# The head of a fused transformer block: value branch on four partitions with a 4 KB load, its copies ahead of the weight casts, attention weights loaded one chunk later

## What is computed

```python
x = x + _L0_attn_a_ref(_layernorm(x), W, b)            # value of token 1, added to every token of its batch
x = x + _L0_ffn_ref(_layernorm(x), W_r, W_k, W_v, mu_r, mu_k)
x = x + _L0_attn_b_ref(_layernorm(x), Wq, bq, Wk, bk, Wv, bv, Wo, bo)
x = x + _L0_ffn_ref(_layernorm(x), W_r, W_k, W_v, mu_r, mu_k)

def _L0_attn_a_ref(x, W, b):
    v = jnp.einsum('btc,dc->btd', x, W) + b
    return jnp.broadcast_to(v[:, 1:2, :], (B, T, C))

def _L0_ffn_ref(x, ...):
    x_prev = x shifted by one token
    xr = mu_r * x + (1.0 - mu_r) * x_prev
    xk = mu_k * x + (1.0 - mu_k) * x_prev
    r = sigmoid(xr @ W_r.T);  k = square(relu(xk @ W_k.T))
    return r * (k @ W_v.T)
```

## Time and profile before

| | us |
|---|---|
| median of three runs | 1783.31 |
| lowest, highest | 1781.94, 1785.71 |
| the profiled execution, whole | 1786.81 |
| its span, first to last instruction | 1785.0 |
| PE busy | 1527.8 |
| DVE busy | 1496.1 |
| ACT busy | 1317.8 |
| POOL busy | 947.9 |

### The profile page before, as it was taken

How to read it: one execution, slowest core, us unless ns; L and a number is a source line. 1 busy time by engine, 2 the same in 40 slices (tenths; PEclk the granted TensorE clock), 3 DMA queues, 4 the chain that set the end, 5 groups by cost and what they waited for, 6 DMA issues and landing times. The chain is left out here.

```text
span 1785.0 us, 46651 instructions
## 1 busy us (share of the span) xinstructions
PE 1527.8 (86%) x16872; PEld 1150.4 (64%) x16872; DVE 1496.1 (84%) x4034; ACT 1317.8 (74%) x2413; POOL 947.9 (53%) x762
## 2 busy tenths in 40 slices
PE   2788865789998989999998989999898999857998
PEld 1677752556666656666666666666666666646887
DVE  3888834889989989999999989999998999826885
ACT  2678823787878768777877878787876877718996
POOL 0243333565656656666665656566665666402444
PEclk8899977989999999999999999999999999978999
DMA  5032211888999899999999999999989998951322
GB/s 191 24 101 74 81 62 47 150 147 151 179 160 178 145 168 162 177 163 161 176 168 167 163 171 170 164 174 170 176 149 170 159 173 154 161 126 49 119 95 84
DMA packets 738435, 252.62 MB, mean 142 GB/s; under 512 B 703776, under 2 KB 722976, under 8 KB 738208
## 3 DMA queue, kind: packets, MB, share of 16 engines
q1 hardware_dynamic: 736688, 248.45, 72.7%
q10 hardware_dynamic: 1520, 1.18, 0.2%
HBM read 48.25 MB, written 25.17 MB: 41 GB/s over the span
## 5 line engine op out<-in xcount | busy, mean ns | idle before, releaser
L1174 ACT ACTIVATE at_prob<-at_prob,at_top 128x256 f32<-128x256 f32 x1024 | 435.8, 497 | 109.0 <-DVE at_top L1042 103.8
L1042 DVE CUSTOM_DVE_ANT_0 at_prob<-at_s_ps,at_masks,pre_s_scale 128x256 f32<-128x256 f32 x1024 | 428.8, 479 | 19.5 <-PE at_s_ps L1392 4.3
L1298 PE MATMUL at_pr_ps<-at_xt,pre_w_h 128*128 128x512 f16 x1024 | 298.9, 384 | 22.5 <-DMA at_xt<-at_x_halves 19.9
L1053 DVE TENSOR_TENSOR at_halves<-at_prob,at_halves 128x1024 f16<-128x1024 f32 x256 | 313.9, 1242 | 2.4 <-ACT at_halves L1184 2.4
L1392 PE MATMUL at_s_ps<-at_kt,at_qt 32*128 32x256 f32 x4096 | 263.3, 393 | 52.1 <-DVE at_top L1042 24.7
L986 POOL TENSOR_TENSOR at_c_halves<-at_ctx,at_c_halves 128x1024 f16<-128x1024 f32 x64 | 136.5, 2132 | 295.4 <-DVE at_halves L1053 288.3
L1392 PEld LDWEIGHTS at_s_ps<-at_kt,at_qt 32*128 32x128 f32 x4096 | 210.9, 188 | 113.4 <-issue 110.7
L1184 ACT ACTIVATE at_halves<-at_prob 128x1024 f16<-128x1024 f32 x256 | 269.6, 1053 | 6.1
L1355 PE MATMUL at_c_ps<-at_v_h,at_pt 128*128 128x65 f16 x2048 | 215.2, 195 | 60.6 <-DMA at_pt<-at_halves 33.4
L1355 PEld LDWEIGHTS at_c_ps<-at_v_h,at_pt 128*128 128x128 f16 x2048 | 187.5, 98 | 120.4 <-issue 58.4
L955 POOL TENSOR_TENSOR at_kt<-at_k_by 128x512 f32<-128x512 f32 x128 | 162.9, 1273 | 110.1 <-DVE at_halves L1053 110.0
(11 more groups left out here) (133 smaller groups left out, 3209.2 us busy)
## 6 DMA issues: line engine op xcount, KB each, us to landing
f_x<-in_x SPq DMA_DIRECT2D x16, 512.0 KB, 4.6
x_after_ffn<-f_x SPq DMA_DIRECT2D x16, 512.0 KB, 3.1
at_x_ln<-x_after_ffn SPq DMA_DIRECT2D x16, 512.0 KB, 4.6
at_x_res<-x_after_ffn SPq DMA_DIRECT2D x64, 128.0 KB, 3.0
x_after_attention<-at_x_res SPq DMA_DIRECT2D x64, 128.0 KB, 3.0
f_x<-x_after_attention SPq DMA_DIRECT2D x16, 512.0 KB, 4.6
out_x<-f_x SPq DMA_DIRECT2D x16, 512.0 KB, 3.0
at_tables<-in_cos SPq DMA_DIRECT2D x16, 256.0 KB, 3.7
```

Source lines behind the costliest of these rows:

```text
L1042: last = nc.vector.tensor_tensor_reduce(out=prob[:, n % 2, h, :], in0=s_ps[:, h, n % 2 * 2 * P:(n % 2 + 1) * 2 * P], in1=masks[:, kind, :] ...
L1053: nc.vector.tensor_tensor(halves[:, n % HB, 1, :, :], prob[:, n % 2, :, :], halves[:, n % HB, 0, :, :], ALU.subtract).then_inc(p_low, 1)
L1174: last = nc.scalar.activation(prob[:, n % 2, h, :], prob[:, n % 2, h, :], ACT.Exp, bias=top[:, n % 2, h:h + 1], scale=-1.0)
L1298: last = nc.tensor.matmul(pr_ps[:, half, :].rearrange("p (b t) -> p b t", b=SB), w[wp][:, k, at:at + P], xt[:, r, xp, :, k, :], start=n == ...
```

## The change

The value rows are loaded once, one batch to a partition: four pieces of 1 KB into `va`. Layer norm runs on [4, 256] with one instruction each in place of four. PE transposes two blocks [4, 128]; a single ACT copy spreads the four columns of each to 128, and stands ahead of the `w_h` cast. The semaphore `consts` is split into `w_in` (W_r, W_k) and `mu_in`; ACT issues the mu loads second and third, ahead of `ba`, W_r and W_k. The products go to `v_ps` and `r_ps` instead of `k_ps` and `v_ps`. Only the first batch's `vb` is written ahead of the loop; the other three are written at the end of iteration -2. `Prepared` issues its six loads in SP's iteration 1 instead of 0, reduces in iterations 2 and 3 instead of 1 and 2, spills, scales and casts one iteration later.

```diff
-                sp.dma_start(xn[:, 0, :, :], x_in[1, 0:NBLK:BPB, :].partition_broadcast(P)).then_inc(value_in, 16)
+                sp.dma_start(va[:, :], x_in[1, 0:NBLK:BPB, :]).then_inc(value_in, 16)
...
-                for j in range(CB):
-                    last = nc.vector.bn_stats(stats[:, 1, j, :], xn[:, 0, j, :])
-                last.then_inc(va_stats, 1)
+                nc.vector.bn_stats(va_moments[:, :], va[:, :]).then_inc(va_stats, 1)
...
             if weights is not None:
-                dve.wait_ge(consts, 16 * 4)
+                dve.wait_ge(mu_in, 32)
                 nc.vector.tensor_scalar(mu_rest[:, :, :], mu[:, :, :], -1.0, 1.0, ALU.mult, ALU.add).then_inc(rest_made, 1)
                 dve.wait_ge(w_high, 1)
...
             if value is not None:
-                for b in range(BATCH):
-                    dve.wait_ge(va_done, b + 1)
-                    nc.vector.tensor_tensor(vb[:, b, :], (k_ps, v_ps)[b // 2][:, b % 2, 0:C],
-                                            ba[:, :], ALU.add).then_inc(vb_made, 1)
+                value_of(0)
...
+                if value is not None and c == -2:
+                    for b in range(1, BATCH):
+                        value_of(b)
                 if side is not None:
                     side.vector(dve, c)
...
+            if weights is not None:
+                wr_t, wk_t, wv_t, mu_r, mu_k = weights
+                act_e.dma_start(mu[:, R, :], mu_r).then_inc(mu_in, 16)
+                act_e.dma_start(mu[:, K, :], mu_k).then_inc(mu_in, 16)
...
-                act_e.wait_ge(consts, 16 * 4)
+            if value is not None:
+                act_e.wait_ge(va_t, 1)
+                nc.scalar.activation(mix[:, 0, :, :].rearrange("p k (b t) -> p k b t", b=BATCH),
+                                     t_ps[:, :, 0:BATCH].unsqueeze(3).broadcast_to([P, CK, BATCH, P]),
+                                     ACT.Copy).then_inc(va_xt, 1)
+            if weights is not None:
+                act_e.wait_ge(w_in, 32)
                 nc.scalar.activation(w_h[:, :, :, :], w_raw[:, :, :, :], ACT.Copy).then_inc(w_high, 1)
-            if value is not None:
-                act_e.wait_ge(va_t, BATCH)
-                for b in range(BATCH):
-                    nc.scalar.activation(mix[:, b // 2, :, (b % 2) * P:(b % 2 + 1) * P],
-                                         t_ps[:, :, b * P:(b + 1) * P], ACT.Copy).then_inc(va_xt, 1)
...
-    SPILL_AT, SCALE_AT = 3, 5
-    CAST_AT = (6, 8, 10, 12)
+    SPILL_AT, SCALE_AT = 4, 6
+    CAST_AT = (7, 9, 11, 13)
 
     def sync(self, sp, c):
-        if c == 0:
+        if c == 1:
...
-        if c in (1, 2):
+        if c in (2, 3):
             dve.wait_ge(self.raw_in, 16 * 6)
```

More of the change, by code:

```diff
@@ L174, in ffn_phase @@
             w_raw = sb("w_raw", [P, 2, CK, C])
-            consts = sem("consts")
+            w_in = sem("w_in")
+            mu_in = sem("mu_in")
             rest_made = sem("rest_made")
@@ L245, in _ @@
                 pool.wait_ge(va_mv, 1)
-                nc.gpsimd.tensor_tensor(veps[:, 1, :], mv[:, 1, :, 1], eps[:, :], ALU.add).then_inc(va_veps, 1)
+                nc.gpsimd.tensor_tensor(va_stds[:, 0:1], va_mean[:, 1:2], eps[0:BATCH, 0:1], ALU.add).then_inc(va_veps, 1)
                 pool.wait_ge(va_veps, 1)
-                nc.gpsimd.tensor_tensor(rstd[:, 1, :], veps[:, 1, :], power[:, :], ALU.pow).then_inc(va_rstd, 1)
+                nc.gpsimd.tensor_tensor(va_stds[:, 1:2], va_stds[:, 0:1], power[0:BATCH, 0:1],
+                                        ALU.pow).then_inc(va_rstd, 1)
             def std_of(c):
@@ L275, in _, with value_of @@
                 dve.wait_ge(value_in, 16)
-                for j in range(CB):
-                    last = nc.vector.bn_stats(stats[:, 1, j, :], xn[:, 0, j, :])
-                last.then_inc(va_stats, 1)
+                nc.vector.bn_stats(va_moments[:, :], va[:, :]).then_inc(va_stats, 1)
                 dve.wait_ge(va_stats, 1)
-                for j in range(CB):
-                    last = nc.vector.bn_aggr(mv[:, 1, j, :], stats[:, 1, j, :])
-                last.then_inc(va_mv, 1)
+                nc.vector.bn_aggr(va_mean[:, :], va_moments[:, :]).then_inc(va_mv, 1)
                 dve.wait_ge(va_rstd, 1)
[L284 to L287, removed]
+                nc.vector.tensor_scalar(va[:, :], va[:, :], va_mean[:, 0:1], va_stds[:, 1:2], ALU.subtract,
+                                        ALU.mult).then_inc(va_xn, 1)
+            def value_of(b):
+                dve.wait_ge(va_done, b + 1)
+                nc.vector.tensor_tensor(vb[:, b, :], (v_ps, r_ps)[b // 2][:, b % 2, 0:C], ba[:, :],
+                                        ALU.add).then_inc(vb_made, 1)
             if weights is not None:
-                dve.wait_ge(consts, 16 * 4)
+                dve.wait_ge(mu_in, 32)
                 nc.vector.tensor_scalar(mu_rest[:, :, :], mu[:, :, :], -1.0, 1.0, ALU.mult, ALU.add).then_inc(rest_made, 1)
@@ L479, in _ @@
                 pe.wait_ge(va_xn, 1)
-                for b in range(BATCH):
-                    for k in range(CK):
-                        last = nc.tensor.transpose(t_ps[:, k, b * P:(b + 1) * P],
-                                                   xn[:, 0, b, k * P:(k + 1) * P], ident[:, :])
-                    last.then_inc(va_t, 1)
-                pe.wait_ge(va_xt, BATCH)
+                for k in range(CK):
+                    last = nc.tensor.transpose(t_ps[:, k, 0:BATCH], va[:, k * P:(k + 1) * P], ident[0:BATCH, 0:BATCH])
+                last.then_inc(va_t, 1)
+                pe.wait_ge(va_xt, 1)
                 pe.wait_ge(wa_in, 32)
@@ L622, in vector @@
         nc = self.nc
-        if c in (1, 2):
+        if c in (2, 3):
             dve.wait_ge(self.raw_in, 16 * 6)
-            for n in (2 * c - 2, 2 * c - 1):
+            for n in (2 * c - 4, 2 * c - 3):
                 nc.vector.tensor_reduce(self.w_max[:, n:n + 1], self.raw[:, n, :], AX.X, ALU.max,
```

16 lines of the change are left out of this document (9 added, 7 removed).

## The result

The changed kernel takes 1789.03 us, median of 20 runs (1779.93 to 1797.42), against 1783.72 for 20 runs of the kernel before on the same chips (1778.74 to 1789.79). The ratio is 1.0029 [1.0016, 1.0043]: 5.3 us slower, just beyond the 3.6 us that can be told from no change. 1778.1 had been predicted, with 1772.5 to 1783.5 as the range. The profiled execution took 1788.79 us, its span is 1787.0.

A forecast was written before the change was run, and what follows sets the result against it. Late DMA loads were taken to bound the head and DVE the loop. Head -15.2, `vb` +0.3, wait +8.7 and drain +0.8 gave -5.4, rounded to -5.2 us: 1778.1 against 1783.31, range 1772.5 to 1783.5.

The forecast's parts named there:

- The head: Before the first chunk: W_k in at about 13.8, `take(0)` at 16.5 instead of 31.71, a gain of 15.2 us.
- The other leg: Value rows through layer norm, ACT's copy and PE's products in the head: first product at about 14, costing nothing.
- The three further `vb`: End of iteration -2, ahead of `moments(1)`: mostly hidden by DVE's idle time, a loss of 0.3 us.
- the wait: DVE in iteration 2, waiting for the later weight loads, complete about 19.7 us into it: a loss of 8.7 us.
- The drain: End of f1: the last cast moves to the end of iteration 14, costing 0.8 us, between 0 and 2.
- the sum: All terms together, -15.2 + 0.3 + 8.7 + 0.8 = -5.4, rounded to -5.2 us.
- The rest: The attention and f2, where the change touches no instruction: no change of time was forecast.
- the signs: What would show the forecast right, among it everything behind shifted by one constant, about 5 us earlier, up to the attention.
- rival 3: Iteration 2: weight loads beside a full pipeline make the wait pass 17.7 us, so the kernel gets slower; chance 7%.

The follow-up runs named there:

- e2: The kernel before with only the attention weights loaded, reduced, spilled and cast one iteration later: ratio 1.0036 to the kernel before.
- e1: The changed kernel with the attention weight loads and the work on them at the iterations of the kernel before: ratio 0.9993 to the kernel before.
- e3: The changed kernel with idle work in the value branch, giving PE, DVE and ACT as many instructions ahead of the attention as before: 1777.95 us, ratio 0.997.
- e8: The changed value branch, weight loads and casts where they were, with idle filling on PE, DVE and ACT: 1774.02 us, ratio 0.9946 to the kernel before.
- e16: A repeat of e8, unaltered: 1773.05 us, ratio 0.9943 to the kernel before.
- e13: The kernel before with its value branch computed for batch 0 alone, taking as many instructions off each stream as the change: 1789.97 us, ratio 1.0038.
- e9: The changed kernel with 9 statistics, 3 activations and 6 transposes added behind the attention, at the head of f2: ratio 1.0017 to the kernel before.
- e10: The kernel before with six more small transposes on PE in the value branch: ratio 0.9981 to the kernel before.
- e14: The kernel before with extra small instructions in the head: six transposes on PE, nine statistics on DVE, three copies on ACT: ratio 0.9982.
- e11: The changed kernel with 128 more small transposes on PE in the head, 256 instructions with their weight loads: ratio 1.0014 to the kernel before.
- e6: The changed kernel with only six extra transposes on PE, DVE and ACT unfilled: ratio 0.9997 to the kernel before.
- e5: The changed kernel unaltered, measured again: ratio 1.0032 to the kernel before.

## Why the prediction was wrong

**The head: right.** W_k was to be in at 13.8 and the cast started at 13.93; `take(0)` was to start at 16.5 and did at 16.68; the gain was to be 15.2 and was 15.0. The other leg was over-costed, with the copy near 12 and the first product near 14: ACT's loads were issued much faster (the copy at 5.60), and the products waited for `ba` until 10.59. They stayed off the path, as said.

**The three further `vb` and the wait: right.** 0.3 + 8.7 were predicted. Iteration 0 starts 15.0 us earlier than before (29.86), iteration 4, behind all reductions in both kernels, 6.7 earlier (92.16 against 98.85 in the earlier trace rows): 8.3 lost, 7.8 of it the idle row. The loads were to be complete 19.7 us into iteration 2, and DVE's reduction began 71.77 - 52.09 = 19.7 us into it. A loss of 6.4 us in the two pairs of whole runs (e2 against before, the changed kernel against e1) is less than those 8.3; the late loads also give something back in the head: `take(0)` at 19.94 in e1 and 16.68 with them, 31.71 before and 28.50 in e2.

**The drain: too small.** 0.8 was taken, with 2 as the upper end. The last cast now comes late:

```profile
228.34 2.35 DVE L665 SCALAR_TENSOR_TENSOR pre_wo_l<-pre_raw,pre_w_up,pre_wo_h 128x2048 f16<-128x2048 f32 x1 [0.86 <-ACT pre_wo_h L673]
```

Iteration 14, which now holds it, took 12.5 us instead of 10.2. Iteration 15 starts at 230.61; from 92.16 to there are 138.5 us, against 134.4 before, and the end of f1 behind it is 1.4 shorter: 2.7 us in sum. So f1 ended 4.0 us earlier where 5.2 were predicted. Up to here the sum held to 1.2 us.

**The rest: wrong, and this is the step that failed.** "The change touches no instruction there or in f2, so I read the rest only where f1 stands", and, among the signs, "everything behind is shifted by one constant, about 5 us earlier, up to the attention". f1 ends so, though its lead wanders between 2.7 and 8.2 us behind iteration 4; the attention isn't shifted so: it gave the 4.0 back and 2.3 more in the profiled executions, and by the medians (5.3 slower, with f1 4.0 faster) it and f2 are 9.3 us longer. No rival held this case: rival 3, the only one that ended on the slow side, put the loss into the wait, which was 7.8 us, not beyond 17.7. The chance of slower was 7%, because every mechanism I listed lay in f1.

What the runs showed in its place: the attention is longer when the few instructions that the change takes off the streams of PE, DVE and ACT are missing ahead of it. Three pairs agree: the changed kernel against e3 (10.5 us), e1 against e8 and e16 (8.4 and 8.9 by the ratios, of which 2.9 and 4.5 lie in f1), e13 against the kernel before (6.8, made by taking instructions off). e9, filled behind the attention, has the long attention (1352.5) and PE's idle time (174.6) of the short streams. That more instructions ahead are better in general is not shown: e10 and e14 gain 0.2% at most, and e11, with 128 more transposes, gains less than e6 with six. When the attention begins does not decide: at 251 to 252 us it was short in e3 and long in e13, near 240 to 242 short, near 245 to 248 long.

With streams of equal length the change does what the sum said: e3 is 5.3 us faster than before, where 5.2 was predicted. That the two agree so well is partly chance, since f1 of e3 ended only 0.8 earlier and the rest came from its attention.

**What stays open** is how the place acts. It comes out most clearly in PE's idle time (173.9 us after, 168.5 before, 166.0 in e3), but not in one wait. That for `at_pt` is 41.6 us after, 33.4 before and 33.5 in e3, yet e1, with an attention as long as the changed kernel's, waits less for it than the kernel before:

```profile
PE at_c_ps L1362 <- DMA at_pt<-at_halves: 31.5, 24, 3.7
```

Nor do the stretches with a granted clock of 0.50, the lower level of 1.2 GHz, sort the runs: over the whole attention they sum to 87.9 us after, 85.8 before, 71.5 in e3 and 93.0 in e5, but 89.1 in e8. Where the difference begins the traces don't show. Instructions themselves arrive by DMA: the page of the changed kernel has 137 transfers of 16 KB on queue q8, and 90 on another queue. That q8 is PE's follows from e11, where 256 more instructions on PE make it 138.

```profile
q8 instruction: 137, 2.24, 0.5%
...
q14 instruction: 90, 0.74, 0.1%
```

Filling may shift the moments at which these fall among the 256 transposes of `at_halves`; no run shows that this is the cause. The Trainium skill, "Runtime: NRT & Kernel Launch", section "Instruction fetch mechanics", says that instructions are refilled in 16 KiB blocks of 256 and that crossing a block is mostly hidden. The size agrees with the row; whether the crossing is hidden here, no run shows. If the place within a block were all, e11, with one whole block more on PE, should have stayed at 1.0029; it came to 1.0014 [1.0004, 1.0024], which neither confirms nor excludes it. PE's idle time, 169.5 us in e11 against 170.4 to 176.9 in the runs with short streams, speaks weakly against it. Against it also speaks that PE, DVE and ACT each give about the same by the ratios.

## What to carry to other kernels

An edit in the first 15% of a program can change the time of an untouched phase behind it by 0.5%, so for an edit worth less than that, measure each phase from boundary to boundary before explaining the total, hold a wait that differs between two traces beside a repeat of each kernel before calling it the cause, and run one control that keeps the instruction counts ahead of the long phase. Moving a load costs the queue's whole backlog at its new place, and that sum can be made to 1 us from the issue rows and the windows. The faster head is worth having without the later loads: 4 KB in place of 512 KB ahead of everything, the loads where they were, and streams as long as before gave 0.9946 and 0.9943, with six instructions more 0.9933.

## What the runs showed of the hardware that was not expected

- When additions on DVE and POOL start 0.08 to 0.09 us apart, the one that starts second takes longer: 2.31 instead of 1.22 us on DVE, 2.29 instead of 1.30 on POOL (iteration 3 of e3 and of the changed kernel).
- 12, 9 and 3 fewer instructions (of PE with its weight loads, DVE, ACT) ahead of a phase of 1350 us lengthened it and what follows by about 9 us in the changed kernel (5.3 + 4.0), and cost 6.8 us in e13.
- A load of 4 KB to four partitions landed 1.5 us after its issue at 0.74; the one of the same rows to all partitions took 9.6. The issue of the load of W_k on ACT fell from 2.12 us to 0.55.
- The weight loads ran at 392 to 424 GB/s with PE and DVE idle (64 to 68 us), and at 397 beside a working PE (60 to 62 us). The Trainium skill, "DMA: Bandwidth & Descriptors", section "Where 436 GB/s comes from", gives about 358 as the limit from HBM for one core: this trace is above it in three of the windows shown, and had I taken the page's figure, the wait would have been forecast 1.4 us longer, further from the 7.8 measured.
